# Four of sixteen relations: rows of x are summed by relation in the first gather and multiplied by W_r afterwards

## What is computed

```python
x = x + rgcn(layernorm(x), ...)      # touched by the change
x = x + moe(layernorm(x), ...)       # 8 experts, capacity 1.25
x = x + gcn(layernorm(x), ...)       # the second gather, same edges
x = x + lstm(layernorm(x), ...)

def rgcn(x):
    deg = max(1, count of edges by (relation, dst))
    h_all = einsum('nd,rdo->rno', x, W_r)
    msg = h_all[edge_type, src] / deg[edge_type, dst][:, None]
    return segment_sum(msg, dst) + x @ W0_w.T + W0_b
```

## Time and profile before

| what | us |
|---|---|
| runs | 4068.09 to 4073.8, median 4069.11 |
| profiled execution, span | 4443.8 |
| relations stage, from 37.6 to 793.5 | 755.9 |
| first gather's stage, from 805.7 to 2016.7 | 1211.0 |
| second gather, from 2525.9 to 3690 | 1164.1 |
| TensorE busy in the span | 3422.0 (77%) |
| VectorE busy in the span | 1898.4 (43%) |
| granted clock of TensorE, mean | 0.855 |

### The profile page before, as it was taken

One profiled execution on the slowest core, in us unless ns is written; L12 is line 12 of the kernel. 1 busy time (PEld: TensorE's weight loads), 2 busy tenths in 40 slices (PEclk: granted clock), 3 DMA queues, 4 the chain that ended last, 5 costly groups with the idle time before them and its releaser, 6 DMA issues. The chain is left out here.

```text
span 4443.8 us, 59668 instructions
## 1 busy us (share of the span) xinstructions
PE 3422.0 (77%) x18753; PEld 2613.4 (59%) x18753; DVE 1898.4 (43%) x5881; ACT 912.0 (21%) x2407; POOL 1686.3 (38%) x1769
## 2 busy tenths in 40 slices
PE   7999999455567666667999554566667779999996
PEld 3444444354556555565666444445555557999996
DVE  4555300133334444454555421223334445544687
ACT  2333333000000111112333200000000002444554
POOL 1000000566666666653222366666666660000000
PEclk9999999677777777778999766777888889999998
DMA  4333444333444545553333323333444444433333
GB/s 148 149 149 149 154 168 164 116 107 110 124 122 144 161 134 148 150 150 108 116 113 110 109 86 94 107 116 122 126 138 146 152 154 147 153 126 119 110 109 113
DMA packets 246926, 580.34 MB, mean 131 GB/s; under 512 B 45059, under 2 KB 130588, under 8 KB 232783
## 3 DMA queue, kind: packets, MB, share of 16 engines
q1 hardware_dynamic: 158816, 334.44, 21.9%
q0 software_dynamic: 85344, 238.92, 18.3%
q10 hardware_dynamic: 2448, 3.15, 0.2%
HBM read 384.29 MB, written 191.42 MB: 130 GB/s over the span
## 5 line engine op out<-in xcount | busy, mean ns | idle before, releaser
L1676 POOL DMA_INDIRECT b_msg<-scratch_gx,k_src_row x782 | 770.6, 985 | 385.2 <-issue 220.0
L941 POOL DMA_INDIRECT a_msg<-scratch_hrel,k_rel_row x782 | 755.1, 966 | 424.1 <-issue 214.8
L717 PE MATMUL r_psm<-k_w,r_xnT 128*128 128x512 f32 x1568 | 696.4, 599 | 10.4 <-ACT k_slab L681 9.5
L1019 PE MATMUL a_ps<-a_hit,a_msg 128*128 128x128 f32 x3128 | 556.5, 343 | 170.6 <-issue 112.9
L1727 PE MATMUL b_ps<-b_hit,b_msg 128*128 128x128 f32 x3128 | 481.2, 317 | 197.3 <-issue 117.9
L1019 PEld LDWEIGHTS a_ps<-a_hit,a_msg 128*128 128x128 f32 x3128 | 501.3, 248 | 209.6 <-issue 137.4
L1727 PEld LDWEIGHTS b_ps<-b_hit,b_msg 128*128 128x128 f32 x3128 | 462.8, 230 | 246.4 <-issue 148.4
L2130 PE MATMUL l_psg<-k_hall,k_whhT 128*128 128x125 f32 x4640 | 550.7, 277 | 5.2 <-DVE k_hall L2256 5.2
L2130 PEld LDWEIGHTS l_psg<-k_hall,k_whhT 128*128 128x128 f32 x4640 | 538.4, 193 | 5.7 <-DVE k_hall L2256 5.7
L717 PEld LDWEIGHTS r_psm<-k_w,r_xnT 128*128 128x128 f32 x1568 | 294.2, 192 | 356.0 <-issue 342.5
L1831 DVE TENSOR_TENSOR k_accT<-k_accT,b_ps 128x256 f32 x196 | 82.6, 422 | 654.2 <-remote 476.0
(11 more groups left out here) (290 smaller groups left out, 4200.4 us busy)
## 6 DMA issues: line engine op xcount, KB each, us to landing
l_xr<-scratch_xrow SPq DMA_DIRECT2D x146, 512.0 KB
scratch_hrel<-k_slab SPq DMA_DIRECT2D x50, 1024.0 KB
scratch_hrel<-r_hst SPq DMA_DIRECT2D x48, 1024.0 KB
scratch_xrow<-n_xs SPq DMA_DIRECT2D x50, 512.0 KB
a_typ<-scratch_typ SPq DMA_DIRECT2D x196, 96.0 KB
a_msg<-scratch_hrel,k_rel_row POOLq DMA_INDIRECT x782
b_msg<-scratch_gx,k_src_row POOLq DMA_INDIRECT x782
n_xb<-scratch_gx SPq DMA_DIRECT2D x48, 256.0 KB
```

What stands on the lines that cost most here:

```text
L717: mm = pe.matmul(psm[:, c % 4], xnT[:, u, kk], k.w[:, kk, c * 512:(c + 1) * 512], start=(kk == 0), stop=(kk == 1))
L941: pool.indirect_dma_start(msg[:, q, j], None, table, bass.IndirectOffsetOnAxis(ap=rows_of[:, g, j:j + 1].bitcast(U32), axis=0)).then_inc(s ...
L1019: mm = pe.matmul(ps[:, u, kk, 0:WIN], msg[:, g % SL, j, kk * P:(kk + 1) * P], hit[:, u, j], start=(j == 0), stop=(j == pieces(g)[-1]))
L1676: pool.indirect_dma_start(msg[:, q, j], None, rows_of, bass.IndirectOffsetOnAxis(ap=k.src_row[:, g, j:j + 1].bitcast(U32), axis=0)).then_i ...
```

## The change

With SUMMED = 4, the last four relations are not multiplied in the relations stage. That stage computes 12 relations, 6 chunks and 24 passes a tile, and also stores the normalised row itself: a row of `hrel` has 13 blocks, twelve products and the row of x. An edge of the last four relations gathers the row of x. In the first gather the matrix `hit` then has five sections (`NS`), one for all multiplied relations and one for each summed one, and so do the sums and the accumulator. Groups are cut into units of 4, 2 or 1 pieces with a window of w nodes, w from 4 to 26:

```diff
+def width(k, p, m):
+    nodes = place(k, (p + m) * P) - place(k, p * P)
+    return -(-int(1000 * (nodes + 2 + 4.5 * nodes / (P * m) ** 0.5)) // 2000) * 2
+def cut_units(k):
+    while p < k.NPC:
+        m = next(m for m, most in ((4, 14), (2, 18), (1, 64)) if p % m == 0 and width(k, p, m) <= most)
...
+        k.units.append((p, m, width(k, p, m)))
```

```diff
                     def sums(g):
...
+                        for n in units_in(g):
+                            c = NS * k.units[n][2]
+                            if n >= 2:
+                                pe.wait_ge(s_add, n - 1)
+                            for j in pieces_of(n):
+                                pe.wait_ge(s_m[g % SL][j], 16 * (g // SL + 1))
+                            for kk in range(2):
+                                for j in pieces_of(n):
+                                    mm = pe.matmul(banks[:, n % 2, kk * c:(kk + 1) * c], msg[:, g % SL, j, kk * P:(kk + 1) * P],
+                                                   hit[:, g % 2, j, 0:c], ...)
+                            mm.then_inc(s_mm, 1)
                     def turn_sums(t):
...
+                        for r in range(SUMMED if along else 0):
+                            for kk in range(2):
+                                pe.matmul(psa[:, 0:D], acc[:, kk * NS + 1 + r, lands(t)], wq[:, kk, r * D:(r + 1) * D],
+                                          start=False, stop=False, skip_group_check=True)
...
+                    def wipe(t):
+                        act.wait_ge(S["tp"], t + 1)
+                        act.copy(acc[:, :, lands(t)], k.zero[:]....broadcast_to([P, 2 * NS, P])).then_inc(S["wi"], 1)
...
                     def add(g):
+                        if k.wiped[g]:
+                            v.wait_ge(S["wi"], k.wiped[g])
+                        for n in units_in(g):
+                            p, m, w = k.units[n]
+                            at = v.value_load(k.at_ring[0:1, p:p + 1], min_val=0, max_val=k.RL - 1)
+                            v.wait_ge(s_mm, n + 1)
+                            if n:
+                                v.wait_ge(s_add, n)
+                            v.tensor_tensor(acc[:, :, bass.ds(at, w)], acc[:, :, bass.ds(at, w)],
+                                            banks[:, n % 2, 0:2 * NS * w]..., ALU.add).then_inc(s_add, 1)
```

```diff
         for_windows(k, "deg", deg.window, ended, lambda: run(True), fresh=k.degT)
+        with nc.If(nc.values_load(k.late[0:1, 0:1], min_val=0, max_val=1) > 0):
...
+            again()
+        nc.all_engine_barrier()
```

In the relations stage SP's stores and VectorE's waits become:

```diff
+                        for a, z in ((0, C1), (C1, NC)):
+                            rest(k, sp, S["ea"], NC * t + z + 4)
+                            sp.dma_start(to[bass.ds(t * P, P), a * 512:z * 512],
+                                         hst[u][:, a * 512:z * 512]).then_inc(s_h[u], 16)
+                            if z == C1 and not full:
+                                sp.dma_start(k.hrel[bass.ds(t * P, P), k.R1 * D:(k.R1 + 1) * D],
+                                             xn[:, u]).then_inc(s_i[u], 16)
...
                         rest(k, v, S["tp"], t + 1)
+                        if not full:
+                            rest(k, v, s_i[s % 2], 16 * (2 * i + s // 2) + 16)
                         ln.rows(v, t, xt[:, s], xn[:, s % 2])
```

More of the change, by code:

```diff
@@ new lines, in again, with _ @@
+        def again():
+            with nc.Block(no_gpsimd_drain=True) as block:
+                @block.vector
+                def _(v):
+                    link = Chain(v, S["re"])
+                    link(v.tensor_copy(table(0), edge(k.src_row)))
+                    link(v.scalar_tensor_tensor(out=table(0), in0=table(0), scalar=R / 2.0, in1=edge(k.typf),
+                                                op0=ALU.mult, op1=ALU.add))
+                    link(v.tensor_copy(edge(k.rel_row), table(0)))
+                @block.sync
+                def _(sp):
+                    for s in range(XR):
+                        sp.dma_start(xt[:, s], x[s * P:(s + 1) * P]).then_inc(s_x[s], 16)
+            run(False, True)
@@ L565, in run @@
+        def run(counted, full=False):
+            NC = (R if full else k.R1) * D // 512
+            C1 = (NC + 1) // 2
+            to = k.hfull if full else k.hrel
+            hst = (k.slab, k.slab if full else second)
             with nc.Block(no_gpsimd_drain=True) as block:
@@ L612, in _ @@
                     pool.wait_ge(S["z"], 2 if counted else 1)
-                    pool.wait_ge(S["f0"], 16)
+                    if not full:
+                        pool.wait_ge(S["f0"], 16)
                 @block.vector
@@ L653, in _ @@
                         deg.inverse_dve(v)
+                        count_odd(v)
                     else:
@@ L709, in turn, with tile @@
                         mm.then_inc(S["tp"], 1)
-                    def tile(t, u, more, groups):
+                    def tile(t, s, more, groups):
+                        u = s % 2
                         rest(k, pe, S["xt"], t + 2)
@@ L780, in stage_first @@
     s_s = [k.sem(f"g_s{u}") for u in range(SR)]
+    s_q = [k.sem(f"g_q{u}") for u in range(XQ)]
     k.s_slab = k.sem("g_slab")
@@ L923, in tiles @@
             ended = lambda g: [b for b, (lo, hi) in enumerate(batches) if begin[hi - 1] == g]
+            units_in = lambda g: range(k.upto[g], k.upto[g + 1])
+            pieces_of = lambda n: range(k.units[n][0] % PER, k.units[n][0] % PER + k.units[n][1])
+            if along:
+                assert all(begin[k.wiped[g] - 1] <= g - 2 for g in range(NG) if k.wiped[g])
             with nc.Block(no_gpsimd_drain=True) as block:
@@ L994, in _ @@
                         sp.wait_ge(s_d[u], 16 * len(range(u, NT, XR)))
-                    sp.wait_ge(S["dx"], 32 * NT)
+                    for u in range(XQ):
+                        sp.wait_ge(s_q[u], 32 * len(range(u, NT, XQ)))
                 @block.tensor
@@ L1277, in _ @@
                     for g in slots:
+                        for t in begun(g):
+                            if along and t and t % RING == 0:
+                                spill(t)
                         if along and g + 2 < NG:
```

282 lines of the change are left out of this document (205 added, 77 removed).

## The result

The changed kernel takes 4486.02 us (4483.88 to 4487.45), the kernel before in the same session 4071.45: a ratio of 1.102, 95% interval [1.1004, 1.1036], or 415 us more. Forecast were 246 more. The profiled execution of the changed kernel has a span of 4482.0, about the time of a run. One execution of the kernel before that was not profiled took 4434.97 (the 4071.45 is the median of all four, 4069.11 that of the other three), so an execution about as long as the profiled one occurs without the profiler too; the ratio leaves it out.

What follows compares the result with a forecast made beforehand. It took the relations stage as bound by TensorE and the unprofiled first gather by GpSimd's pace. From 4069 us, −94 for the relations stage and +341 for the first gather gave 4316, said as 4315, range 3980 to 4430.

Steps and rivals of the forecast that it cites:

- The gathers' pace: First gather, unprofiled: GpSimd sets the pace, 5.02 us a group; 359 of the trace's 375 us excess are gather stalls.
- So the ordinary group costs nothing: First gather from group 76: VectorE's 4.5 us a group of four units stays under GpSimd's 5.02, adding nothing.
- The tile's chain: First gather, group where a tile ends: engines wait in turn, 11.0 us between last matmuls; at 42 tiles +283 at full clock.
- the quarter that was guessed: First gather: a quarter of the tiles run at TensorE's lower clock, 5.6 us more each, giving +341 instead of +283.
- The free tiles: Relations stage, free part: 24 passes take 10.53 us a tile instead of 13.96; 21 tiles give 72 less.
- The dip: Relations stage, inverses: TensorE's 9.49 us idle grows by 5, with `count_odd`'s reduce by 6, leaving −66 for the free part.
- the row's store: Relations stage: one more DMA per tile on SP for the normalised row, taken as 0; 147 if late by 3 us a tile.
- The counted tiles: Relations stage, 28 tiles: VectorE's own chain becomes late next, 14.4 us a tile instead of 15.82, −39.
- Starts and ends: Relations stage: +3 for edge loads, +4 ahead of the first LayerNorm, +4 for the extra branch with its barrier.
- (B): First gather: the tile's chain is overlapped and only the relations stage counts, 3975 us; chance 0.25.
- (C): First gather: TensorE's low clock throughout, +518, total 4493 us; chance 0.08.
- (D): Whole kernel: the parts cancel, 4069 us, with the chain 5.9 us shorter than reckoned; chance 0.06.

Runs made afterwards that it cites:

- e1b_relations: Kernel before with 12 relations in the relations stage and a 12-row table, without row's store, windows or extra branch: 3985.29 us, ratio 0.979 to the kernel before.

## Why the prediction was wrong

Its direction and its mechanism held: the kernel is slower because in the first gather the engines wait for each other in turn, above all where a tile ends, and GpSimd's pace is lost from about group 90 on. The time lies outside the range, by 56 us.

- **The gathers' pace, right.** 5.02 a group was worked out from the earlier trace rows; `e1b_relations` shows 5.08. Taking the 375 us as stalls outside the program fits too: that run's two gathers take 991 and 1001, against 1176 and 1147.
- **"So the ordinary group costs nothing", wrong: the step that failed.** The 4.5 us counted VectorE's work alone. weigh has a register load for each unit, which the text named in its list of the change's parts but never costed on TensorE; they stand in series on its queue and made the group 6.0, over GpSimd's 5.02. Moved away, the group takes 4.2, and 106 us come back. By the table the groups between two tiles' groups take 6.7 + 0.86 × 6.0 = 11.9 where the forecast had 1.86 × 4.5 = 8.4; 3.5 more at 42 tiles are 147, about the 136 by which the stretch from first to second gather was missed.
- **The tile's chain, near in its sum and off in its parts.** 12.2 was measured; the forecast had 11.0 at the higher clock, and 12.4 with a quarter of its 5.6 for the lower one. The passes were as forecast: line L1215 is busy 238.2 us in 49 tiles, 4.9 a tile, between 4.1 and 7.6 at the quarter that was guessed. The sums were not: the forecast gave them the same quarter, and 1483 of 1839 of their passes began at the lower level of 1.2 GHz. A unit took 1.02 there, half of 2.05, against the forecast's 0.5 and 0.9; that the sum still came out is luck in part.
- **The free tiles, right to 0.01 us.** The dip was forecast 6 longer and came 20 longer (29.45 against 9.49): the text put the row's store at 0 because it has half a tile to land, and did not look where SP's queue stands at the inverses, though it named the queue. Four buffers gave 16 back.
- **The counted tiles, half right.** VectorE is late next, as said; but a tile takes 15.0 with the first half alone and 15.4 in the changed kernel, not 14.4: −12 in place of −39. What the 0.4 between the two are is not shown; four row buffers left them.
- **Starts and ends** came to +7 at the start (7 forecast); the first gather begins 18.2 after the start of the last L862 in the changed kernel, against 13.4 after that of L717, with the branch between: 5, where 4 were forecast.
- **The rivals.** (B), that the chain is hidden, did not happen. (C), the low clock throughout, gave 4493, and the time came near it by luck: its chain would be 16.6 and was 12.2, and loads and relations stage made up what the clock did not cost. (D), that the parts cancel, did not happen either.

What stays open: why the clock was granted at 0.60 in one kernel and 0.93 in others, and how the tail behind the last gather could be shortened: from there to the experts' stage it takes 85 us in the kernel with wider units, against 35 in `e1b_relations`, more than the 27 by which that kernel is slower than the kernel before.

## What to carry to other kernels

When a step is cut into more units, list for each engine what one unit issues, register loads too, and add it up on that engine's own queue; here a load was free behind the sixteen passes and in the open between weigh's short matmuls, 0.76 us for each. Narrow windows save columns, but a unit's price here was its load, its hand-off and its add: the adds came 0.8 to 0.9 us apart with 220 elements and with 400. So cut as coarsely as the bank allows; up to windows of 44 nodes that paid. Before a new store is called hidden, look at the worst moment of its queue, not at the average one.

## What the runs showed of the hardware that was not expected

- A pass of L1019 or its like takes 0.128 us with 128 columns and took 0.256 with 110 columns in the changed kernel (eight in 2.05): fewer columns, and slower, at the lower clock (granted 1.00 from 1036 to 1038.1 and 0.50 from 1943 to 1948). At 1.00 the passes with 110 columns took 0.143 (eight in 1.14).
- TensorE busy 342 us of 370 with a granted clock of 0.62, and busy 287 of 370 with 0.93: between these two kernels the busier one had the lower clock.
- Register loads of 0.30 us, with what stands around them in the queue, come 0.76 apart. The Trainium skill, page "DMA: Bandwidth & Descriptors", section "Latency and other measured facts", gives a `tensor_load` a floor of some 600 ns; the traces of this case disagree for the load itself (median 304 ns on VectorE's queue, and 301 on TensorE's in the changed kernel), while the spacing of loads in a row lies above it.
